# Opening of a conditioned four-layer convolution kernel rebuilt: reciprocal root from the table, static sums on TensorE, more of the next groups' work ahead of the loop

## The reference

```
def _layer(x, style, w, b, mw, mb, typ):
    s = style @ mw.T + mb
    weight = SCALE * w * s[:, None, :, None]
    demod = lax.rsqrt(jnp.sum(weight * weight, axis=(2, 3)) + EPS)
    weight = weight * demod[:, :, None, None]
    ...
x = x + _L0_cond_ref(x, cond_512, ...)     # layers: same, upsample + blur, same, blur + downsample
```

## Time and profile before

| what | value |
|---|---|
| median of 3 runs | 692.41 us (690.55 to 693.0) |
| the profiled execution | 691.5 us, of which its span is 689.6 us |
| PE busy | 660.8 us (96%) |
| DVE busy | 471.3 us (68%) |
| POOL busy | 374.0 us (54%) |
| ACT busy | 313.0 us (45%) |
| DMA | 117.22 MB, mean 170 GB/s |

### The profile page before, as it was taken

One profiled execution on the slowest core, in us unless ns is written; L12 is line 12 of the kernel. 1 busy time (PEld: TensorE's weight loads), 2 busy tenths in 40 slices (PEclk: granted clock), 3 DMA queues, 4 the chain that ended last, 5 costly groups with the idle time before them and its releaser, 6 DMA issues.

```text
span 689.6 us, 12124 instructions
## 1 busy us (share of the span) xinstructions
PE 660.8 (96%) x4434; PEld 618.8 (90%) x4434; DVE 471.3 (68%) x705; ACT 313.0 (45%) x499; POOL 374.0 (54%) x392
## 2 busy tenths in 40 slices
PE   5668999999999999999999999999999999999997
PEld 4667899999999999999999999999999999999986
DVE  6867668777675687676757786757666967586551
ACT  3424534544544445454444444444444543545441
POOL 3355555755555646646565555566555565655420
PEclk9989999999999999999999999999999999999999
DMA  7054767876767867756787757678776576877763
GB/s 246 0 116 79 188 179 176 205 179 144 180 170 189 207 146 184 183 157 179 187 207 177 166 145 194 161 194 207 177 175 157 156 190 182 207 177 177 167 156 137
DMA packets 130234, 117.22 MB, mean 170 GB/s; under 512 B 6080, under 2 KB 96576, under 8 KB 130176
## 3 DMA queue, kind: packets, MB, share of 16 engines
q1 hardware_dynamic: 129520, 114.88, 66.7%
q10 hardware_dynamic: 656, 1.57, 0.7%
HBM read 36.47 MB, written 33.82 MB: 102 GB/s over the span
## 4 chain that ended last, share of the span: by engine, by line
PE 95%; DVE 3%; issue 1%; ACT 1%; DMA 1%; POOL 0%; DVEq 0%; POOLq 0%; ACTq 0%
PE po L174 17%; PE po L175 16%; PE po L176 16%; PE pg L174 8%; PE pg L176 8%; PE pg L175 8%; PE pg L179 4%; PE pg L180 4%; PE pm L176 3%; PE pm L174 3%; PE pm L175 3%; PE pe L378 1%; PE pe L371 1%; DMA Gf<-in_st 1%; PE pe L381 0%
## 5 line engine op out<-in xcount | busy, mean ns | idle before, releaser
L174 PE MATMUL po<-xh,W 128*128 128x256 f32 (+1 forms) x640 | 218.2, 341 | 2.4 <-DVE T L682 1.7
L175 PE MATMUL po<-xl,W 128*128 128x256 f32 (+1 forms) x640 | 217.6, 340 | 0.0
L176 PE MATMUL po<-xh,W 128*128 128x256 f32 (+1 forms) x640 | 217.4, 340 | 0.0
L176 PEld LDWEIGHTS po<-xh,W 128*128 128x128 f32 x640 | 126.2, 197 | 12.3
L174 PEld LDWEIGHTS po<-xh,W 128*128 128x128 f32 x640 | 125.6, 196 | 12.3 <-issue 2.7
L175 PEld LDWEIGHTS po<-xl,W 128*128 128x128 f32 x640 | 126.1, 197 | 9.9
L602 POOL TENSOR_TENSOR Q2l<-Q2f,Q2h 128x512 fp32r<-128x512 f32 x31 | 74.0, 2386 | 85.5 <-ACT Q2h L489 85.5
L682 DVE SCALAR_TENSOR_TENSOR T<-po,DD,M 128x512 f32<-128x512 f32 x64 | 48.0, 750 | 82.6 <-PE po L176 51.0
L450 ACT CAST xh<-X 128x1032 fp32r<-128x1032 f32 x64 | 80.9, 1264 | 37.9 <-PE po L176 37.9
L673 DVE TENSOR_TENSOR xl<-X,xh 128x1032 fp32r<-128x1032 f32 x64 | 95.9, 1499 | 2.4 <-ACT xh L450 2.4
L494 ACT CAST Gh<-Gf 128x512 fp32r<-128x512 f32 x64 | 39.8, 621 | 119.0 <-DVE Gf L704 119.0
(11 more groups left out here) (169 smaller groups left out, 1523.2 us busy)
## 6 DMA issues: line engine op xcount, KB each, us to landing
X<-in_xin SPq DMA_DIRECT2D x64, 516.0 KB, 4.4
out<-T SPq DMA_DIRECT2D x64, 512.0 KB, 3.5
W<-W SPq DMA_DIRECT2D x96, 256.0 KB, 4.3
W<-W SPq DMA_DIRECT2D x32, 384.0 KB, 5.6
V<-V SPq DMA_DIRECT2D x32, 128.0 KB, 5.1
V<-W SPq DMA_DIRECT2D x32, 64.0 KB, 3.6
V<-Vx SPq DMA_DIRECT2D x32, 64.0 KB, 2.8
E<-in_ed ACTq DMA_DIRECT2D x1, 768.0 KB, 7.4
```

The lines of the kernel that those rows point to most:

```text
L174: eng.matmul(o, wh_, rh, start=first, stop=False)
L175: eng.matmul(o, wh_, rl, start=False, stop=False)
L176: return eng.matmul(o, wl_, rh, start=False, stop=last)
```

## The change

The reciprocal root comes from one ScalarE activation (`Abs_reciprocal_sqrt`) in place of a root there and a reciprocal on VectorE; the Newton step is written in three instructions, and `D32` comes from a side branch of it. The sums of B1 are made by 18 exact f32 matmuls on TensorE: the identity times 1, 6, 15 or 20 (`EK`) against slices of `b1t`, added up in PSUM in the banks `po[0]` and `po[1]`, from which ScalarE and VectorE take them. The scale matmuls come in two halves, the input DMAs are issued in another order and most of them on SP. Units (1, 2) and (1, 3) move ahead of the loop with `conv(0)`, `x_low(1)` and the group-2 preparation of `Q3`; the rests of `Q2` and `G` of group 1 are computed on VectorE and not on GpSimd; group 0's cross copy is issued for two samples at a time (`cross_pair`), and `FIRST` is gone, so that the first group has the same slots as the others. A helper `warm` is defined but not called; the fill of `WARM`, for which the first matmul waits, is one memset on GpSimd.

```
-PROLOGUE = [(0, 0), (0, 1), (0, 2), (0, 3), (0, 4), (0, 5), (0, 6), (1, 0), (1, 1)]
-FIRST = [[(1, 2), (1, 3)], [(1, 4), (1, 5), (1, 6)], [(2, 0), (2, 1)], [(2, 2), (2, 3)]]
+PROLOGUE = [(0, u) for u in range(7)] + [(1, u) for u in range(4)]
...
+            def cross_pair(a):
+                w = r32(W[:, 0]).rearrange("p v t a r m -> p (v t) a r m")
+                s = s_wb if a else s_w[0]
+                for part, (i, e, f) in enumerate(((0, 4, 4), (4, 10, 8))):
+                    sp.wait_ge(s_wh, part + 1)
+                    sp.wait_ge(s_wl, part + 1)
+                    sp.dma_start(w[hi, i:e, a, 1], w[lo, i:e, a, 0]).then_inc(s, 16)
+                    sp.dma_start(w[lo, i + 2:f + 2, a, 1], w[hi, i:f, a, 0]).then_inc(s, 16)
...
-            cross(0, 0)
-            cross(0, 1)
+            cross_pair(0)
+            cross_pair(1)
...
+                def add(c, i, n, rhs, first, last=False):
+                    return pe.matmul(pb[d][:, i:i + n], EK[c][p, at], rhs, start=first, stop=last)
...
+            pe.wait_ge(s_dm, 1)
+            pe.wait_ge(s_in["mw2"], 16)
+            pe.wait_ge(s_in["st"], 16)
+            scales(P2)
+            scales(P3).then_inc(s_pp, 1)
             pe.wait_ge(s_sq, 1)
             pe.wait_ge(s_sc, SC_SQ2)
             energy(2).then_inc(s_pp, 1)
+            pe.wait_ge(s_in["mwt"], 16)
+            scales(0)
+            scales(1).then_inc(s_pp, 1)
+            pe.wait_ge(s_in["b1"], 16)
+            pe.wait_ge(s_ek, 3)
+            static_sums(0).then_inc(s_bp, 1)
             pe.wait_ge(s_sq, 2)
-            pe.wait_ge(s_ss, 1)
+            pe.wait_ge(s_ss, 2)
             for l in (0, 1, 3):
                 m = energy(l)
...
+            static_sums(1).then_inc(s_bp, 1)
...
             constant(2, 1, SC_K2)
+            conv(0)
+            constant(3, 3, SC_K3)
...
-            act.activation(one[:], one[:], ACT.Sqrt)
+            act.activation(one[:], one[:], ACT.Abs_reciprocal_sqrt)
...
+            q3_high(2)
+            high(1, 2)
+            high(1, 3)
             sums_high(0)
+            x_high(1)
...
-            low(1, 0)
-            low(1, 1)
+            pool.wait_ge(s_wl, 2)
             x_parts(1)
+            q3_full(2)
+            q3_low(2)
...
-            def newton(l):
-                link(tt(tmp[:, l], RR[:, l], RR[:, l], ALU.mult))
-                link(tt(tmp[:, l], tmp[:, l], AA[:, l], ALU.mult))
-                link(dve.tensor_scalar(tmp[:, l], tmp[:, l], -0.5, 1.5, ALU.mult, ALU.add))
-                link(tt(DD[:, l], tmp[:, l], RR[:, l], ALU.mult))
+            def newton(l, t, also=None):
+                link(tt(t, RR[:, l], AA[:, l], ALU.mult))
+                if also:
+                    tt(kt[:], RR[:, l], also[0], ALU.mult)
+                link(dve.scalar_tensor_tensor(out=t, in0=t, scalar=-0.5, in1=RR[:, l], op0=ALU.mult, op1=ALU.mult))
...
-            link(dve.reciprocal(RR[:, 0:3], RR[:, 0:3]))
```

More of the change, by code:

```diff
@@ L125, in build @@
         ST = flat3(Gf, 512, 512 + B)
[L126 to L130, removed]
+        EK = [EYE[:]] + [flat3(Wf, 256 * k, 256 * k + 256) for k in range(3)]
+        WARM = xl[:, 1, 0, 0:640]
         Y1 = flat(AA, 0, 13 * EC).rearrange("p (b n) -> p b n", n=13)
@@ L234, in cross_sums @@
                 sp.dma_start(v[lo, 1, :, 1], r32(Vx[hi])).then_inc(s_v[g % 2], 16)
-            for n in range(XR):
-                load(n)
+            load(0)
+            load(1)
+            sp.dma_start(E[:], ed.rearrange("p (l t m) -> p l t m", l=4, t=3)).then_inc(s_in["ed"], 16)
+            load(2)
             sp.dma_start(XE[:], xe).then_inc(s_in["xe"], 16)
-            cross(0, 0)
-            cross(0, 1)
+            cross_pair(0)
+            cross_pair(1)
             cross_sums(0)
@@ L382, in edge, with warm, scales @@
                 m.then_inc(s_e, 1)
[L384 to L388, removed]
+            def warm(n, at):
+                for _ in range(n):
+                    pe.matmul(at[:, :], WARM[:, 0:128], WARM[:, 128:640], start=True, stop=True)
+            def scales(l):
+                return pe.matmul(ps[:, l * 128:l * 128 + 128], MW[:, l, :], ST, start=True, stop=True)
             def energy(l):
@@ L416, in _ @@
             pe.wait_ge(s_cl, 1)
-            for x in PROLOGUE[4:9]:
+            for x in PROLOGUE[4:]:
                 unit(*x)
@@ L430, in _ @@
                     edge(*edge_at[divmod(b - 1, NG)])
[L431 to L433 removed]
+                if b:
+                    conv(b)
         @block.scalar
         def _(act):
[L437 to L439 removed]
+            for n, dst, src in (("st", ST, st), ("wt2", WT[:, 2], wt.rearrange("p (l t m) -> p l t m", l=4, t=3)[:, 2]),
+                                ("eye", EYE[:], eye)):
                 act.dma_start(dst, src).then_inc(s_in[n], 16)
@@ L554, in _ @@
                         sums_high(x[0])
-                if b == 0:
-                    q3_high(2)
-                    x_high(1)
-                if i >= 2:
+                if i >= 2 and not (b == 2):
                     m_out(b)
@@ L832, in _ @@
-            reached(tt(D32[:], DD[:, P2], S[:, P3], ALU.mult))
+            dve.wait_ge(s_pp, 3)
+            reached(tt(S[:, 0:2], psv[:, 0:2], bc(BB[:, 1, 0:2], B), ALU.add))
+            dve.wait_ge(s_sc, SC_S1)
+            dve.wait_ge(s_ss, 1)
+            link(newton(P2, tmp[:, P2], (S[:, P3], D32[:])))
             dve.wait_ge(s_sc, SC_D32)
@@ L891, in _ @@
             reached(tt(tmp[lo, 3], kt[lo], S[lo, P3, :], ALU.mult))
+            g_low(1)
+            sums(0)
+            sums_low(0)
             for b in range(B):
```

187 lines of the change are left out of this document (101 added, 86 removed).

## The result

The changed kernel takes 684.6 us (median of 4 runs, 683.42 to 686.34) against 691.97 us (4 runs, 690.55 to 693.0): ratio 0.990, with a 95% interval of 0.987 to 0.993. 684.5 had been forecast. The profiled execution took 686.34 us with a span of 684.5, and before 691.5 with 689.6. So the pair of profiles shows 5.1 us of the gain of 7.4 between the medians: of the missing 2.2, 1.7 come from the profiled execution after the change, which was the slowest of its four, and 0.5 from the one before.

A forecast was written before the change was run, and what follows sets the result against it. TensorE never idles from 74 to 660 us, so only its 22.9 us not busy before 74 and its low clock count. Landmark gains reach 7.4 at conv(4): 691.5 - 7.4 = 684.1, stated as 684.5, range 679 to 689.5.

The forecast's parts named there:

- The opening: Start to unit (0, 0): time taken from VectorE is spent on TensorE's sums; start at 16.2, 0.3 us later.
- I take 3.4: First nine sum matmuls on TensorE: 3.1 us if 64 columns cost half, 4.0 if the same; 3.4 taken.
- weights that don't overlap: Rival at the exact sums: each record costs 0.55 us, 19.8 and not 6.9; time 698; chance 0.03.
- the root needed no other table: Rival on ScalarE's root: table switches at 1.28 us each, five of them 6.4, about 691 us; chance 0.02.
- To (1, 2): Unit (0, 4) to (1, 2): Q2 between W's rests, its rest on VectorE, later x split; 37.7, 3.45 us won.
- The collision: Before (1, 2): GpSimd's x subtractions hold VectorE's instructions; price 0.65 us, between 0 and 1.3.
- The forecast of 44.1: Start of conv(0): 24 matmuls at the low clock, 5.1 us, and K2 in six records, 1.3, after (1, 2).
- both cases: Opening's clock: stays low (684.5 us, chance 0.51) or rises early (680.5 us, chance 0.3); both may occur.
- The rival's conv(4), 62.4: Clock high from about 12.3 us in the opening: conv(4) at 62.4, gain 11.2, time 680.5; chance 0.3.
- the clock that stays high: Units (1, 2) and (1, 3) at the high clock: 2.2 us more, gain 8.6 and not 6.4; middle 7.4 taken.
- Conv(4): Start of conv(4): group 1's W copies end last, SyncE no longer held; 67.2 for 73.57, gain 6.4, raised to 7.4.
- The W term: VectorE's last rest of group 1's W before conv(4): done at 60.3, 1.9 us later than before.

The follow-up runs named there:

- The short sums: Changed kernel with five of the nine matmuls of each B1 sum left out (output differs): 683.45 us, ratio 0.986.
- `xparts_early`: Changed kernel with GpSimd's two subtractions on the second pair of x moved ahead of its wait for D: 683.01 us, ratio 0.988.
- `xlow1_late`: Changed kernel with the split of the second pair of x put back behind `constant()`: 687.95 us, ratio 0.994.

## Why the prediction came out right

**The opening: right.** (0, 0) at 16.28 with no wait, because the microseconds taken from VectorE are spent on TensorE. The short sums confirm it with 3.9 us. Two terms were off and cancelled, which is luck. The first scales ran at 3.51 and not 4.33, so that the sums began at 8.27 and not 8.9; and the sums were mis-sized: "I take 3.4" and 3.5 for 9 matmuls each, which took 3.9 (8.27 to 12.14) and 4.1 us (18.71 to 22.84). The upper bound of 4.0, "if they cost the same", was the fitting one. Hence the 0.7 us at (0, 2) was not won. The chance of 0.03 for weights that don't overlap is refuted: 0.215 a record, not 0.55. And the root needed no other table: each of the two traces has a single table load.

**To (1, 2): right in size and mechanism.** 37.62 against 37.7. The collision was put at 0.65 between 0 and 1.3; the half-height rest alone lost 0.79 (1.21 against 0.42), while the one before it lost nothing (0.67 against 0.69), although by the profile GpSimd had begun 0.13 us ahead of it. There it was GpSimd that paid: its first subtraction took 1.76 us, where the same form takes 1.10 at 16.30 in `xparts_early`, 0.66 more, about the length of VectorE's rest of 0.67. So it seems that of two such instructions one waits for the other; the spans on GpSimd are rough, and no run tests which of them has to. The split of x, at 37.51, also took 2.02 where the form takes 1.23 alone. By the Trainium skill (GPSIMD Engine Reference, Specifications) GpSimd shares its SBUF interfaces with VectorE and contends with VectorE's instructions of two SBUF inputs; the trace agrees (1.21 us beside GpSimd, 0.42 alone).

At conv(0) 1.96 of the 3.53 us are left: K2's six records now stand ahead of it (1.10 us), and the 24 matmuls took 5.39 us, all at the low level, where before the change the level rose at 45.8, ahead of the last two of them, and the whole way took 4.92. The forecast of 44.1 had both terms, 5.1 and 1.3, right in their sum.

**The clock: both cases occur.** Low through (1, 2) and (1, 3) in the first profile, early in the traces of `xparts_early` and `xlow1_late`, whose edits lie behind the opening. The rival's conv(4), 62.4, was met by the 62.89 of the first; its time of 680.5 was met by no run of the changed kernel, the ten of which lie between 681.4 and 687.7, and the 682.3 of `xparts_early` has 1.6 us in it that were given back at the end. The forecast of 684.5 sits in the middle of a mixture. For an execution like the profiled one the prediction's sum says 684.1, and it took 686.3, 1.3 of it by the later conv(4) and 1.0 because the forecast had gone half-way to the clock that stays high; so the 0.1 us between forecast and median is partly luck. The Trainium skill (TensorE: Matmul & The Clock Gate, part 1) has the number of slow matmuls differ from run to run, and the traces agree (2.27 and 4.21 us for the same 18 records).

**Conv(4): the number right, one step of the reason wrong.** The copy of group 1's W does end last there, before and after, by the landings. What failed is the weight given to it, and with it to the held SyncE: before the change TensorE itself was busy until 72.96 and waited 0.61, so that no earlier copy could have given more than that. Nor was it "the last place where TensorE waits": there is the 1.7 us for T near the end, in both kernels. The kernel before with SyncE freed gained nothing that its runs can show. What had made TensorE late was the sum of what lay ahead, with the wait of 3.3 us before conv(2), and it was this that `x_low(1)` ahead of `constant()` removed, as the prediction also has it. Once TensorE is earlier, the copies count again: after the change it waits 0.95 us for them. The W term itself was good: last rest done at 60.97 (60.3 forecast), conv(4) at 68.50 (67.2). It held TensorE for 0.95 us only, where "a wait of 1 to 2 us" was announced, because TensorE came at 67.55 and not at 65.5; the last copy was issued at 62.18 and landed 6.1 us later. Of these 2 us, 1.28 are the new wait before conv(3): ScalarE makes conv(2)'s M (62.53) only behind the split of the next pair (61.59), and where two units stood between conv(2) and conv(3) there is now one. The prediction counted TensorE's work there and not what M waits for. Another 0.5 us were lost already at conv(2), 57.70 where 57.2 follows from its terms.

**Worth in parts**, in means: the split of x before `constant()` 4.3 us, the rests of Q2 on VectorE 1.7 (1.0 in the traces), the root 1.2 (nothing in the trace), the pair-wise copy 0, of which only the first is clear of the spread; the sums cost about 4 us of TensorE in return for the wait that they fill. These overlap and don't add up. What the move of (1, 2) and (1, 3) gives alone, and whether the change of the input DMAs' order gave the earlier first scales, had no run.

## What to carry to other kernels

When work moves from a waiting engine's supplier to the waiting engine, compare the work that is added with the wait that goes: here 8 us of sums on TensorE filled waits of 2.3 and 4.5 and moved the landmark by nothing, and a change of which only one move (a split issued before a long run of VectorE's work) carries most of the gain looks like a success of all its parts. Ask at a late landmark first whether the engine waits or merely arrives late; the length of a stall on a DMA queue (18.05 us here, whose removal gave nothing that the runs can show) says little of it. And where TensorE idles before a stretch of small matmuls at the low clock, fillers in the hole are cheap: they gave 2.6 us here in the mean, and 2.55 in the trace.

## What the runs showed of the hardware that was not expected

- An exact f32 matmul with 64 columns costs what one with 128 costs at the low clock: 18 records, eight of them of 64 columns, took 3.87 us, 0.215 each, and a record of 128 alone 0.213.
- The clock of the opening differs between executions whose instructions are the same up to there: 2.27 or 4.21 us for the same energies. Before the change, energies over 64 rows from 7.68 to 13.6 us hadn't raised it; after it, neither did 7 us of work from 9 to 16 us in the first profile, where the pace rose at 26.6 us with TensorE at work, gaps of a fraction of a us aside, since 5.71; in other executions it rose at 10.7, 20.2 and 22.8. Fillers from 1.42 us on shift the mean by 2.1 to 2.2 us and guarantee nothing: one profile with them is low, one is high.
- An early clock can be lost again in the opening: low from 17.8 to 24.4 us behind a wait of 1.59 us, and from 24.7 to 28.0 behind one of 1.45.
- The wait of 1.8 us for T near the end can cost the clock too (granted 0.77, 0.73, 0.66 in a stretch of 5 us around or behind it), and then 1.5 to 1.9 us: in three of the traces, while the others keep it.
- Beside GpSimd's work VectorE's subtractions took 1.21 us in place of 0.42, 2.02 in place of 1.23 and 1.59 in place of 0.69; and GpSimd's own took 1.76 in place of 1.10 where VectorE's lost nothing.
